# A macaron transformer layer on eight cores: the LayerNorm squares moved to GpSimd, the softmax denominators of two heads taken together, and x loaded first

## What is computed

```python
def _L0_ffn_ref(x, weight, disha):
    result = jnp.einsum('bsd,od->bso', x, weight)
    pooled = x.reshape(*x.shape[:-1], x.shape[-1] // r, r).sum(axis=-2)
    return result + pooled @ disha

# attention, 16 heads of 64, latent width L = 32
q_lat = q @ q2l_w.T + q2l_b            # k_lat, v_lat likewise with kv2l_w
q_lat = q_lat * cos + _rotate_half(q_lat) * sin        # k_lat likewise
q_for_k = q_lat @ wqk_w.T + wqk_b
att = softmax(where(causal, einsum('bhql,bhkl->bhqk', q_for_k, k_lat) * L**-0.5, -inf))
y = (att @ v_lat) @ l2o_w.T + l2o_b
out = y @ cproj_w.T + cproj_b

x = x + 0.5 * _L0_ffn_ref(_layernorm(x), weight, disha)
x = x + attn(_layernorm(x))
x = x + 0.5 * _L0_ffn_ref(_layernorm(x), weight, disha)
```

## Time and profile before

| | us |
|---|---|
| runs shown | 5707.81 and 5748.43 |
| median | 5728.12 |
| the profiled execution | 5759.79 |
| its span, first to last instruction of the slowest core (core 7) | 5758.2 |
| spans of the other cores | 5691.0 to 5728.0 |

### The profile page before, as it was taken

How to read it: one execution, slowest core, us unless ns; L and a number is a source line. 1 busy time by engine, 2 the same in 40 slices (tenths; PEclk the granted TensorE clock), 3 DMA queues, 4 the chain that set the end, 5 groups by cost and what they waited for, 6 DMA issues and landing times.

```text
span 5758.2 us, 60182 instructions; the slowest of 8 cores (5691.0 to 5758.2 us)
## 1 busy us (share of the span) xinstructions
PE 3720.4 (65%) x13322; PEld 1161.5 (20%) x13322; DVE 1948.4 (34%) x4094; ACT 1934.1 (34%) x2450; POOL 314.4 (5%) x500
## 2 busy tenths in 40 slices
PE   0017665677766666577875667567885766567786
PEld 0002221122211211122221222122221222122222
DVE  1115432532134433351122633253122543254113
ACT  0001351137711162117741144114751135113771
POOL 0001001100011000100001000100001100110000
PEclk9997767777877757676676766677776776677877
DMA  2252003210032102310013101310003210321002
GB/s 64 74 148 59 30 13 89 67 44 1 1 91 72 50 1 73 79 50 12 1 51 89 55 19 39 98 53 23 1 26 99 59 30 13 90 68 42 1 1 77
DMA packets 152675, 281.45 MB, mean 49 GB/s; under 512 B 34466, under 2 KB 34466, under 8 KB 152354
## 3 DMA queue, kind: packets, MB, share of 16 engines
q1 hardware_dynamic: 124962, 214.67, 12.7%
q0 software_dynamic: 8960, 29.37, 3.1%
q10 hardware_dynamic: 18432, 33.56, 1.6%
HBM read 235.59 MB, written 46.14 MB: 49 GB/s over the span
## 4 chain that ended last, share of the span: by engine, by line
PE 46%; DVE 16%; issue 15%; ACT 12%; DMA 8%; POOL 1%; SPq 1%; DVEq 1%; ACTq 0%; POOLq 0%
PE PS L897 11%; PE PS L858 9%; PE PS L616 9%; PE PS L683 7%; ACT PT L870 5%; PE PS L990 4%; DVE ln_sb L598 3%; DMA stg<-w_attn 3%; DVE rb_sb L942 3%; DMA out<-out_stg 3%; ACT r_sb L921 2%; PE PS L559 2%; PE PS L564 2%; DVE out_stg L625 1%; ACT r_bf L924 1%
## 5 line engine op out<-in xcount | busy, mean ns | idle before, releaser
L870 ACT ACTIVATE PT<-PS,b_exp 128x1024 bf16<-128x1024 f32 (+7 forms) x1536 | 1256.8, 862 | 535.5 <-PE PS L858 498.2
L858 PE MATMUL PS<-q_store,k_store 32*128 32x512 bf16 (+3 forms) x2560 | 752.7, 437 | 206.4 <-DVE rb_sb L942 110.1
L555 ACT ACTIVATE sq_sb<-xb_sb 128x512 bf16<-128x512 bf16 x384 | 239.5, 629 | 1855.3 <-POOL xb_sb L552 1393.0
L897 PE MATMUL PS<-PT,v_store 128*65 128x512 bf16 (+3 forms) x2560 | 835.1, 442 | 19.6 <-DVE PT L876 8.5
L616 PE MATMUL PS<-ln_sb,wslot 128*128 128x512 bf16 x2048 | 726.8, 500 | 129.8 <-DVE ln_sb L602 124.3
L876 DVE TENSOR_TENSOR PT<-PT,causal_sb 128x128 bf16<-128x128 bf16 x1024 | 230.6, 225 | 1389.0 <-ACT PT L870 1379.6
L683 PE MATMUL PS<-ln_sb,wslot 128*128 128x512 bf16 x2048 | 643.4, 462 | 83.9 <-DVE ln_sb L602 83.9
L552 POOL CAST xb_sb<-x_sb 128x512 bf16<-128x512 f32 x384 | 252.6, 663 | 4429.8 <-DVE x_sb L1000 2639.4
L559 PE MATMUL PS<-xb_sb,ones_sb 128*1 128x512 bf16 x384 | 167.5, 436 | 485.9 <-POOL xb_sb L552 485.9
L897 PEld LDWEIGHTS PS<-PT,v_store 128*65 128x65 bf16 x2560 | 285.2, 129 | 489.6 <-issue 398.7
L616 PEld LDWEIGHTS PS<-ln_sb,wslot 128*128 128x128 bf16 x2048 | 225.9, 117 | 605.0 <-issue 518.9
(11 more groups left out here) (105 smaller groups left out, 2139.6 us busy)
## 6 DMA issues: line engine op xcount, KB each, us to landing
wslot<-me_strm SPq DMA_DIRECT2D x256, 256.0 KB, 2.6
wslot<-wa_strm SPq DMA_DIRECT2D x256, 256.0 KB, 2.5
wslot<-cp_strm SPq DMA_DIRECT2D x128, 256.0 KB, 2.8
out<-out_stg ACTq DMA_DIRECT2D x128, 256.0 KB, 3.6
x_sb<-x POOLq DMA_DIRECT2D x112, 256.0 KB, 5.1
stg<-w_attn SPq DMA_DIRECT2D x48, 256.0 KB
wa_strm<-build_sb SPq DMA_DIRECT2D x16, 256.0 KB
stg<-ffnT SPq DMA_DIRECT2D x8, 512.0 KB
```

The lines of the kernel that those rows point to most:

```text
L555: p.op("scalar", lambda eng, c=c, par=par: eng.activation(sq_sb[:, TTA * par:TTA * par + TTA], xb_sb[:, TTA * c:TTA * c + TTA], AF.Square) ...
L858: hg=hg, gq=gq: eng.matmul(PS[:, 1024 * par + a:1024 * par + bnd], k_store[32 * hg:32 * hg + 32, seq * gq + 128 * c:seq * gq + 128 * c + 128],
L870: eng.activation(PT[:, QW * slot + qoff:QW * slot + QW], PS[:, 1024 * par + qoff:1024 * par + QW], AF.Exp, bias=b_exp[:, 0:1]),
L897: yb=yb: eng.matmul(PS[0:65, yb + a:yb + bnd], v_store[:, 1040 * c + 65 * h:1040 * c + 65 * h + 65], PT[:, QW * slot + a:QW * slot + bnd], ...
```

## The change

- The LayerNorm square (L555) is a multiply on GpSimd where it was an activation on ScalarE.
- The logarithm and the exponential of the softmax denominators are taken once for both heads of a pair, over 2048 columns, after the second head's last product.
- The cosine and sine tables come as bf16 and are loaded into their place; the two casts go.
- The x of the first half-sequence is loaded before everything else; its load at the later place goes.
- The ring of store semaphores has eight entries for four.
- Scratch is saved: `sd_f` goes and `var_f` is used in place, `disha_sb` shares memory with `ln_sb`, and the mask `maskbig_sb` is neither kept nor loaded. `r_sb` is twice as wide.

```diff
@@ semaphores @@
-                dma = "ST%d" % (self.st_ctr % 4)
+                dma = "ST%d" % (self.st_ctr % 8)
@@ tables, host and DRAM @@
-        cos4=cos4, sin4=sin4,
+        cos4=cos4.astype(BF), sin4=sin4.astype(BF),
-    d_cos4 = dram("cos4", [128, seq])
-    d_sin4 = dram("sin4", [128, seq])
+    d_cos4 = dram("cos4", [128, seq], BF16)
+    d_sin4 = dram("sin4", [128, seq], BF16)
@@ tiles @@
-    sd_f = sb("sd_f", [1, TTA], F32)
-    r_sb = sb("r_sb", [1, QW], F32)
+    r_sb = sb("r_sb", [1, 2 * QW], F32)
-    maskbig_sb = sb("maskbig_sb", [128, 128], BF16)
-    disha_sb = sb("disha_sb", [128, D], BF16)
+    disha_sb = ln_sb
@@ before the first small load @@
+    for o in range(NCH):
+        p.op("sync", lambda eng, o=o: eng.dma_start(
+            out=x_sb[:, HALF * o:HALF * o + HALF],
+            in_=d_x[0, 128 * o:128 * o + 128, 0:HALF]),
+            writes=[p.R("x", o, tt) for tt in range(NT)], dma="LDI")
...
-    ld(maskbig_sb[:], d_maskbig, p.R("maskbig"))
@@ ln_stats_chunk @@
-        p.op("scalar", lambda eng, c=c, par=par: eng.activation(
+        p.op("gpsimd", lambda eng, c=c, par=par: eng.tensor_tensor(
             sq_sb[:, TTA * par:TTA * par + TTA],
-            xb_sb[:, TTA * c:TTA * c + TTA], AF.Square),
+            xb_sb[:, TTA * c:TTA * c + TTA],
+            xb_sb[:, TTA * c:TTA * c + TTA], ALU.mult),
             reads=[p.R("xb", c)], writes=[p.R("sq", par)])
@@ ln_finish @@
-            sd_f[:], var_f[:], AF.Ln, bias=eps_sb[0:1, 0:1]),
+            var_f[:], var_f[:], AF.Ln, bias=eps_sb[0:1, 0:1]),
...
-            a_bf[:], sd_f[:], AF.Exp, scale=-0.5),
+            a_bf[:], var_f[:], AF.Exp, scale=-0.5),
@@ emit_attn_pair, after the last pv_chunk @@
+        yball = [BK[4], BK[6]] + ([BK[5], BK[7]] if QW > 512 else [])
+        p.op("scalar", lambda eng: eng.activation(
+            r_sb.ap().rearrange("p (s w) -> p s w", w=QW)[0:1, 0:2, :],
+            PS.ap().rearrange("p (s w) -> p s w", w=1024)[64:65, 2:4, 0:QW],
+            AF.Ln),
+            reads=yball, writes=[p.R("r")])
+        p.op("scalar", lambda eng: eng.activation(
+            r_bf[:, 0:2 * QW], r_sb[:, 0:2 * QW], AF.Exp, scale=-1.0),
+            reads=[p.R("r")], writes=[p.R("rbf", 0), p.R("rbf", 1)])
+
         def mk_epilogue(h):
...
-            p.op("scalar", lambda eng, yb=yb: eng.activation(
-                r_sb[:], PS[64:65, yb:yb + QW], AF.Ln),
-                reads=ybanks, writes=[p.R("r")])
-            p.op("scalar", lambda eng, par=par: eng.activation(
-                r_bf[:, QW * par:QW * par + QW],
-                r_sb[:], AF.Exp, scale=-1.0),
-                reads=[p.R("r")], writes=[p.R("rbf", par)])
@@ start of a half-sequence @@
-                ld(stg[:, 0:HALF], dsrc[:, HALF * hb:HALF * hb + HALF],
-                   p.R("stg"))
-                p.op("vector", lambda eng, dd=ddst: eng.tensor_copy(
-                    dd[:], stg[:, 0:HALF]),
-                    reads=[p.R("stg")], writes=[p.R(nm)])
+                ld(ddst[:], dsrc[:, HALF * hb:HALF * hb + HALF], p.R(nm))
...
-            if not pf:
+            if not pf and not (b == 0 and hb == 0):
```

More of the change, by code:

```diff
@@ L42 @@
     CONS_DMA = ("LDI0", "LDI1", "LDI2", "LDI3", "LDI4", "LDI5",
-                "ST0", "ST1", "ST2", "ST3", "PF0", "PF1", "PF2", "PF3",
-                "PF4", "PF5", "PF6", "PF7")
+                "ST0", "ST1", "ST2", "ST3", "ST4", "ST5", "ST6", "ST7",
+                "PF0", "PF1", "PF2", "PF3", "PF4", "PF5", "PF6", "PF7")
     SEM_NAMES = ("LDI0", "LDI1", "LDI2", "LDI3", "LDI4", "LDI5",
-                 "ST0", "ST1", "ST2", "ST3", "PF0", "PF1", "PF2", "PF3",
-                 "PF4", "PF5", "PF6", "PF7",
+                 "ST0", "ST1", "ST2", "ST3", "ST4", "ST5", "ST6", "ST7",
+                 "PF0", "PF1", "PF2", "PF3", "PF4", "PF5", "PF6", "PF7",
                  "PE", "DV", "AC", "PL",
@@ L377, in build_program @@
     ld(stg[:, 0:1024], d_disha2, p.R("stg"))
-    p.op("vector", lambda eng: eng.tensor_copy(disha_sb[:], stg[:, 0:1024]),
+    p.op("vector", lambda eng: eng.tensor_copy(disha_sb[:, 0:1024], stg[:, 0:1024]),
          reads=[p.R("stg")], writes=[p.R("disha")])
@@ L516, in build_program @@
         p.op("vector", lambda eng: eng.tensor_tensor(
-            build_sb[:], stg[:, 0:1024], disha_sb[:], ALU.add),
+            build_sb[:], stg[:, 0:1024], disha_sb[:, 0:1024], ALU.add),
             reads=[p.R("stg"), p.R("disha")], writes=[p.R("build")])
@@ L581, in ln_finish @@
         p.op("scalar", lambda eng: eng.activation(
-            sd_f[:], var_f[:], AF.Ln, bias=eps_sb[0:1, 0:1]),
-            reads=[p.R("var"), p.R("eps")], writes=[p.R("sd")])
+            var_f[:], var_f[:], AF.Ln, bias=eps_sb[0:1, 0:1]),
+            reads=[p.R("var"), p.R("eps")], writes=[p.R("var")])
         p.op("scalar", lambda eng: eng.activation(
-            a_bf[:], sd_f[:], AF.Exp, scale=-0.5),
-            reads=[p.R("sd")], writes=[p.R("a_bf")])
+            a_bf[:], var_f[:], AF.Exp, scale=-0.5),
+            reads=[p.R("var")], writes=[p.R("a_bf")])
         p.group("tensor", [lambda eng: eng.matmul(
@@ L1096, in build_program @@
         break
-    for s in ("ST0", "ST1", "ST2", "ST3"):
+    for s in ("ST0", "ST1", "ST2", "ST3", "ST4", "ST5", "ST6", "ST7"):
         p.raw_wait("scalar", s, p.cnt[s])
```

## The result

| | before | after |
|---|---|---|
| median, us | 5732.58 | 5846.98 |
| lowest to highest | 5707.81 to 5786.24 | 5799.51 to 5870.39 |
| runs | 10 | 11 |
| slowest core's span in the profiled execution | 5758.2 | 5845.3 (core 3) |

After to before is 1.019, 95% interval 1.0153 to 1.0227: the kernel became 1.9% slower, 114 us. The interval lies wholly above 1 and on both sides of 1.02, so a loss is certain, and whether it reaches 2% is not. The forecast was 5747 us, range 5690 to 5825; the measured time is 22 us above its end.

A forecast was written before the change was run, and what follows sets the result against it. The prediction held that no engine is full and hand-overs between engines bound the kernel. Its terms summed to +18, say +19 with roundings, giving 5779 us on the profiled 5759.8 and 5747 us against the median 5728.1; range 5690 to 5825.

The forecast's parts named there:

- The failed step: Attention, denominators of a pair together: doubled activations end about 0.2 us earlier a pair, 56 x -0.2 = -11 us.
- Rounds of the second FFN: Second FFN rounds with prefetch: the square on GpSimd makes each 0.47 us longer, 70 x 0.47 = +32 us.
- the clock rival: Second FFN: longer pauses lower TensorE's clock, +29 us, giving 5776 us; chance 15%.
- Tails: Second FFN, from first to second tile: casts and multiplies alternate on GpSimd, +1.8 in each of 7 sections, +12 us.
- the ends of a half: End of a half-sequence: bf16 tables need no sine cast on VectorE, -0.8 x 7 = -5 us.
- Last half: Last half-sequence, no prefetch: squares on GpSimd escape ScalarE's queue behind the store, 4.3 us a round, -12 us.
- Start: Kernel start: with x loaded first, the first real matmul comes earlier, -14 us (-20 to -5).
- The last pair of each half: Attention's end: the four last VectorE instructions wait for both reciprocals and the projection for them, +2.05 x 8 = +16 us.
- Edits at nothing: Store semaphores, scratch and mask edits, first FFN and attention input projection: covered or about equal, no cost.
- the fourth rival: Eight normalising loops: VectorE blocked by GpSimd for whole multiplies, +19 us, giving 5766 us; chance 10%.

The follow-up runs named there:

- e11: The changed kernel with the last pair's denominators in each half taken head by head, the other seven pairs merged; 5781.50 us, ratio 1.0084 to before.
- e7: The changed kernel with one useless 96-column activation on ScalarE behind each pair's doubled exponential; 5799.07 us, ratio 1.0113 to before.
- e15: The changed kernel with two useless 96-column activations on ScalarE behind each pair's doubled exponential; 5766.18 us, ratio 1.0063 to before.
- e6: The changed kernel without the merge, denominators exactly as before with one shared scratch; 5732.88 us, ratio 0.9999 to before.
- e2: The kernel before with the square on GpSimd, and separate denominators using a half of `r_sb` per head; 5813.25 us, ratio 1.0149.
- e3: The kernel before with x first and bf16 tables, and separate denominators using a half of `r_sb` per head; 5736.43 us, ratio 1.0018.
- e4: The changed kernel without the merge, separate denominators using a half of `r_sb` per head; 5767.37 us, ratio 1.0064 to before.

## Why the prediction was wrong

**The failed step is the merge's.** "The next pair's exponentials, and the broadcast behind them, follow this end: 56 x -0.2 = -11 us." The doubled activations take 1.87 and 1.91 as said, and the fast pair went from 41.26 to 40.94, -0.3 against the -0.2. What the step left out is that 116 matmuls in a pair take 31.9 or 40.6 us by the granted clock, and that the length of the pair bears on how long either lasts. The second halves cost +53 us where the step had about +3 (-5 for 28 pairs, +8 for four ends). Rows that could have warned were there to be read: the pairs of before already differed by 3.5 us at equal work. I had the clock as a rival, but only in the second FFN, at +29 and 15%.

**Rounds of the second FFN.** Forecast +32, measured +46, the growth of the second FFN in the seven halves with prefetch less that of their tails. The terms inside: multiply 1.04 (1.2 was taken; the 1.1 estimated from the Trainium skill, GPSIMD Engine Reference, section 3.1, was nearer), wait on the own engine 0.21 (0.10 was taken). The two errors cancel, which was luck: from the cast to the square's matmul it is 2.11 on the mean of the rounds (2.17), 0.45 more than before, 70 times that is the 32. This part had the mechanism right. The mean round went from 7.55 to 8.24 though, 0.24 more than the chain adds. Most of that is the group of eight matmuls, 3.51 us on the mean where it was 3.32: in before more groups ran partly at 2.4 GHz, while in the round shown of after it takes 3.59. That is the clock rival, at +14 instead of its +29.

**Tails.** From the start of the last eviction of tile 0 to the variance it went from 6.89 to 8.48, +11 over seven (forecast +12). At the ends of a half 9.34 to 8.55, -6 (-5). Right.

**Last half.** Forecast -12, measured -15 for the whole second FFN of that half: rounds of tile 0 went from 5.4 to 6.2 down to 3.6 to 4.0 (4.3 was taken), its tail from 5.28 to 2.74.

**Start.** Forecast -14. The first matmul of the first FFN starts at 411.1 on the mean of the cores where it was 425.4, as forecast (core 3: 409.80, beside the earlier trace rows); by the end of that FFN's first tile it is -18.

**The last pair of each half.** Forecast +16; the first halves show 8.6 for four, and e11 takes just that back; in the second halves the epilogue itself is 2.3 us longer (2.05 was taken). On top the output projection lost 0.6 to 2.0 us in each of its eight places, for which I had nothing: +11 in all, +5 on cores 4 to 7, and +6 and +7 in the merged e7 and e15, which have no clock of 0.81.

**Edits at nothing.** First FFN and input projection: +5 in all, -7 on cores 4 to 7. VectorE blocked by GpSimd, the fourth rival, did not come.

**The sum.** 46 + 11 - 6 - 15 - 18 + 8.6 + 53 + 11 + 5 = +96 by the stages, on the mean of the cores (+85 on cores 4 to 7), against 114 in the medians and 87 between the two spans. The mean of the cores over all executions is 5801 in after and 5703 to 5708 in before on four chips, +93 to +98; the rest of the 114 is the slowest core, 46 us above that mean in after and 25 to 33 in before. Without the 53 and the 11 it would be +32, 5760 to 5765 by the medians: inside the range.

**What stays open.** Why a pair takes one clock pattern and not another, and so why 41.2 falls back to the fast one and 40.9 may hold the slow one. That patterns persist more with short pairs than with long ones is shown by the table behind e15, on one trace for each run; what lies beneath is not. The length is not all of it either: pairs of before and e6 are equally long, yet e6 had 10 at 0.57 and before none; those of e2, e3 and e4 are equally long too, yet e2, whose attention starts as late as that of before, had 4 and the others 30 and 19. Whether the start decides which pattern a short pair falls into is not tested. And whether a half of after falls into the good or the bad pattern was not told apart.

## What to carry to other kernels

Price an edit inside a repeating loop not by its chain alone: list the granted clock of each repetition first, and if equal work already comes in different lengths, any change of the period, a saving too, can cost more than it gives. When parts of a change are tested one by one, keep names and scratch of the undone part exactly as they were. And before an operation is moved to a faster or freer engine, see what stands in front of it in its queue: emitting the statistics ahead of the blocked eviction gave 282 us, and the choice of engine for the square then made no difference that could be told (3 us).

## What the runs showed of the hardware

- Equal pairs of heads take a few distinct lengths, which go with the granted clock: 41 us at 0.83, 43 at 0.74, 44 at 0.69 to 0.77, 46 at 0.61 to 0.65, 47.8 at 0.57. In after they can persist over a whole half: six of 32 halves are at 0.83 throughout.
- Two useless activations of 274 ns behind each pair, 128 in all, made after 81 us faster between the medians.
- GpSimd multiplies 128x512 bf16 with itself in 1.04 us (1033 to 1038 ns as a rule), 1.7 times its cast of the same size, and waits 0.21 us for its own result.
- Twelve fill matmuls a pair raised the slowest core's mean granted clock from 0.700 to 0.743 without any gain in time.
